# Choosing the tokens of eight experts: all at once before the expert stage, or one at a time, the next one's inside it

## The reference, cut to what matters

```python
logits = xf @ Wr + br                     # xf: 16384 x 512, 8 experts
Sm = softmax(logits, axis=-1)
G_t, idx_t = top_k(Sm.T, k)               # each expert takes its k = 16384/8 = 2048 best tokens
tokens = xf[idx]
mid = silu(einsum('keh,ehf->kef', tokens, W_up[group]) + b_up[group])   # F = 1365, a W_up for each pair of experts
out = einsum('kef,efh->keh', mid, W_down) + b_down
y = zeros_like(xf).at[idx].add(G[..., None] * out)
```

## Time and profile before

| | |
|---|---|
| time, median of 3 runs | 3380.66 us (3379.59 to 3381.59) |
| the profiled execution | 3389.43 us, of which 3387.7 us lie between its first and last instruction (the span) |
| PE busy | 3026.1 us, 89% of the span |
| DVE busy | 1734.5 us, 51% |
| ACT busy | 1279.6 us, 38% |
| POOL busy | 1204.9 us, 36% |
| mean granted TensorE clock | 0.953 |

### The profile page before, as it was taken

One profiled execution on the slowest core, in us unless ns is written; L12 is line 12 of the kernel. 1 busy time (PEld: TensorE's weight loads), 2 busy tenths in 40 slices (PEclk: granted clock), 3 DMA queues, 4 the chain that ended last, 5 costly groups with the idle time before them and its releaser, 6 DMA issues.

```text
span 3387.7 us, 58238 instructions
## 1 busy us (share of the span) xinstructions
PE 3026.1 (89%) x23738; PEld 2422.8 (72%) x23738; DVE 1734.5 (51%) x3966; ACT 1279.6 (38%) x2861; POOL 1204.9 (36%) x1100
## 2 busy tenths in 40 slices
PE   4898989989898710699999999999999999999998
PEld 3677777767677510588888888888888788788886
DVE  4788887888887759233333433333332333433432
ACT  4678787887878620111111211111211211211210
POOL 3556565565656433222222221222222222312221
PEclk8899999999999855799999999999999999999999
DMA  3233334333333230222322421322322313312311
GB/s 105 75 115 120 133 114 135 115 131 113 126 127 114 89 96 0 53 38 41 78 37 48 98 45 31 80 43 48 91 41 34 81 39 64 88 31 36 72 31 24
DMA packets 145476, 252.19 MB, mean 74 GB/s; under 512 B 35600, under 2 KB 36624, under 8 KB 145208
## 3 DMA queue, kind: packets, MB, share of 16 engines
q1 hardware_dynamic: 107432, 172.37, 15.2%
q0 software_dynamic: 32768, 67.72, 11.6%
q10 hardware_dynamic: 5008, 8.36, 0.9%
HBM read 137.82 MB, written 102.24 MB: 71 GB/s over the span
## 4 chain that ended last, share of the span: by engine, by line
PE 58%; DMA 1%; issue 0%; POOL 0%; DVE 0%; ACT 0%; POOLq 0%; ACTq 0%
PE UP L1446 28%; PE DN L1472 28%; PE TT L1429 2%; DMA w_raw<-in_L_ffn_W_down 0%; DMA idx<-list_scratch,slots 0%; DMA xg<-rows_scratch,idx 0%; POOL idx L1353 0%; POOL out_x L1378 0%; POOL xg L1362 0%; DVE down_lo L1070 0%; ACT z L1402 0%; ACT down_hi L1064 0%; DVE y L1517 0%; DVE xT_lo L1481 0%; DVE mid_lo L1499 0%
## 5 line engine op out<-in xcount | busy, mean ns | idle before, releaser
L1378 POOL DMA_INDIRECT out_x<-y,idx x128 | 202.0, 1578 | 1282.7 <-DVE y L1519 1282.7
L1402 ACT ACTIVATE z<-UP,bup 128x512 f32<-128x512 f32 (+1 forms) x352 | 240.9, 686 | 867.7 <-PE UP L1446 826.7
L1472 PE MATMUL DN<-down_hi,mid_hi 128*128 128x512 f32 x1408 | 566.7, 402 | 0.0
L1446 PE MATMUL UP<-xT_hi,up_lo 128*128 128x512 f32 (+1 forms) x1408 | 556.1, 395 | 0.0
L1446 PE MATMUL UP<-xT_hi,up_hi 128*128 128x512 f32 (+1 forms) x1408 | 553.6, 393 | 1.6 <-DVE xT_lo L1481 1.5
L1446 PE MATMUL UP<-xT_lo,up_hi 128*128 128x512 f32 (+1 forms) x1408 | 552.4, 392 | 0.0
L1472 PE MATMUL DN<-down_hi,mid_lo 128*128 128x512 f32 x1280 | 505.7, 395 | 0.0
L1472 PE MATMUL DN<-down_lo,mid_hi 128*128 128x512 f32 x1280 | 505.5, 395 | 0.0
L1517 DVE TENSOR_TENSOR y<-DN,bdn 128x512 f32<-128x512 f32 x128 | 88.5, 692 | 732.4 <-PE DN L1472 732.4
L1497 DVE CAST mid_hi<-z 128x512 fp32r<-128x512 f32 (+1 forms) x352 | 149.8, 426 | 504.8 <-ACT z L1402 504.8
L1389 ACT ACTIVATE xT_hi<-TT 128x512 fp32r<-128x512 f32 x128 | 76.4, 597 | 793.9 <-PE TT L1429 793.9
(11 more groups left out here) (244 smaller groups left out, 4974.8 us busy)
## 6 DMA issues: line engine op xcount, KB each, us to landing
xs<-in_x SPq DMA_DIRECT2D x32, 1024.0 KB, 8.2
kraw<-in_ctx SPq DMA_DIRECT2D x32, 1024.0 KB, 6.8
out_x<-xs SPq DMA_DIRECT2D x32, 1024.0 KB, 5.6
rows_scratch<-xfb SPq DMA_DIRECT2D x32, 1024.0 KB, 4.3
w_raw<-in_L_ffn_W_down SPq DMA_DIRECT2D x40, 512.0 KB
w_raw<-in_L_ffn_W_up SPq DMA_DIRECT2D x16, 682.5 KB
mid_hi<-mid_hi ACTq DMA_DIRECT2D x32, 86.0 KB
mid_lo<-mid_hi ACTq DMA_DIRECT2D x32, 84.0 KB
```

What stands on the lines that cost most here:

```text
L1378: pool.indirect_dma_start(out_rows, bass.IndirectOffsetOnAxis(ap=idx[:, n % 2, t:t + 1].bitcast(U32), axis=0), y[:, t, :], None, compute_o ...
L1402: act.activation(z[0:r, k % 2, :], UP[k % 3][0:r, :], ACT.Silu, bias=bup[0:r, e // 2, f:f + 1]).then_inc(s["z"], 1)
L1446: mm = pe.matmul(UP[k % 3][0:r, :], weights.up[wa][:, c, f * P:f * P + r], xT[xa][:, c, :], start=first, stop=(c == CH - 1 and wa == 1))
L1472: mm = pe.matmul(DN[m % 2][:, :], lhs, rhs, start=first, stop=(f == FCH - 1 and lhs is parts[-1][0]))
```

## The change

`choose` is gone, with its block, the two DRAM tensors and the lists of token numbers. A class `Select` inside `experts` chooses the tokens of one expert in 39 steps; a step is one PE part (`product`) and one DVE part (`decide`), which hand over to each other by the semaphores `asked` and `answered`. The gate values of one expert are 128x128, straight from a PE transpose of `sm_all`. The steps are: `turn`; 14 `upper` and 16 `lower` rounds; `ties`; `base` (how many were chosen in earlier partitions); and six `rows` steps, for three tiles of 128 slots each (the last for one). In a round PE multiplies the counts by a matrix of 2^40, so that the sum is far below or above, and DVE clamps it between the two possible next candidates (`ends`). In a `rows` step PE multiplies a 0/1 matrix (`within`: the partition in which a slot lies) by the places in order, and DVE counts how many places lie before the slot; that count is the token number, written to `slots` in SBUF.

The 39 steps of expert 0 stand at the start of the stage on PE and DVE. Those of expert e + 1 stand inside expert e's DN parts: at the chunks f = 2, 4, 6 and 8 of each `t`, so 16 in a block, in the expert's first three blocks. POOL now makes the constants, takes the `lo` of the first ten weight pieces, and only then gathers for block 0; its gathers and its adds to `out_x` take the token numbers from `slots`. SP's eight loads of biases now stand between the first two weight pieces and the other eight. ACT takes the ten `hi`, loads its table, turns the first rows, and then issues the three small moves of `lay`.

```diff
--- before
+++ after
+class Select:
...
+        self.steps = [("turn", 0)] + [("upper", k) for k in range(self.TOP_BIT - self.LOWER, -1, -1)] \
+            + [("lower", k) for k in range(self.LOWER - 1, -1, -1)] + [("ties", 0), ("base", 0)] \
+            + [("rows", g) for g in range(len(self.groups))]
...
+    def constants(self, pool):
+        step = Chain(pool, self.made)
+        step(pool.memset(self.huge[:, :], self.HUGE))
+        step(pool.memset(self.less[:, :], -float(self.K) / P))
+        step(pool.memset(self.less[0:1, :], 0.5 - float(self.K) / P))
+        step(pool.memset(self.ahead32[:, :], 1.0))
+        step(pool.tensor_copy(self.onesb[:, :], self.ahead32[:, :]))
+        step(pool.affine_select(out=self.ahead32[:, :], in_=self.ahead32[:, :], compare_op=ALU.is_gt, fill=0.0, base=0,
+                                pattern=[[1, P]], channel_multiplier=-1))
+        pool.tensor_copy(self.ahead[:, :], self.ahead32[:, :]).then_inc(self.made, 1)
+        pool.iota(self.places[:, P:P + 1], pattern=[[0, 1]], base=0, channel_multiplier=P, allow_small_or_imprecise_dtypes=True)
+        pool.iota(self.slot_end[:, :], pattern=[[P, self.KC]], base=1, channel_multiplier=1, allow_small_or_imprecise_dtypes=True)\
+            .then_inc(self.made, 1)
+        pool.iota(self.slot_row[:, :], pattern=[[1, self.K]], base=0, channel_multiplier=0, allow_small_or_imprecise_dtypes=True)\
+            .then_inc(self.made, 1)
+    def product(self, pe, e, i):
+        kind, g = self.steps[i]
+        bank, pc = self.bank, self.bank[:, 511:512]
+        if e or i:
+            pe.wait_ge(self.asked, len(self.steps) * e + i)
+        if kind == "turn":
+            mm = pe.transpose(bank[:, 0:P], self.sm_all[:, :, e], self.ident[:, :])
+        elif kind in ("upper", "lower"):
+            mm = pe.matmul(pc, self.huge[:, :], self.count[:, :], start=True, stop=True)
+        elif kind == "ties":
+            pe.matmul(pc, self.onesb[:, :], self.tot[:, :], start=True, stop=False)
+            mm = pe.matmul(pc, self.ahead[:, :], self.ties[:, :], start=False, stop=True)
+        elif kind == "base":
+            mm = pe.matmul(pc, self.ahead[:, :], self.taken[:, :], start=True, stop=True)
+        else:
+            for j in range(len(self.groups[g])):
+                mm = pe.matmul(bank[:, j * (P + 1):(j + 1) * (P + 1)], self.within[g % 2][:, j * P:(j + 1) * P], self.places[:, :],
+                               start=True, stop=True)
+        mm.then_inc(self.answered, 1)
+    def reach(self, dve, values, cand, bit):
+        dve.tensor_scalar(self.hit[:, :], values, cand[:, :], self.less[:, :], ALU.is_ge, ALU.add, accum_out=self.count[:, :])\
+            .then_inc(self.asked, 1)
+        half = float(1 << (bit - 1)) if bit else 0.0
+        dve.tensor_scalar(self.ends[:, 0:1], cand[:, :], -half if bit else -1.0, None, ALU.add)
+        self.step(dve.tensor_scalar(self.ends[:, 1:2], cand[:, :], half, None, ALU.add))
+    def lie_within(self, dve, g):
+        first, n = self.groups[g][0] * P, len(self.groups[g]) * P
+        row = self.slot_row[:, first:first + n]
+        self.step(dve.tensor_scalar(self.begun[:, 0:n], row, self.base[:, :], None, ALU.is_ge))
+        return dve.scalar_tensor_tensor(out=self.within[g % 2][:, 0:n], in0=row, scalar=self.past[:, :], in1=self.begun[:, 0:n],
+                                        op0=ALU.is_lt, op1=ALU.mult)
+    def decide(self, dve, e, i):
+        kind, g = self.steps[i]
+        bank, pc = self.bank, self.bank[:, 511:512]
+        if self.step is None:
+            self.step = Chain(dve, self.own)
+        step = self.step
+        halves = self.V[:, :].bitcast(U16)
+        upper, lower = halves[:, 1:2 * P:2], halves[:, 0:2 * P:2]
+        dve.wait_ge(self.answered, len(self.steps) * e + i + 1)
+        if kind == "turn":
+            step(dve.memset(self.cand[0][:, :], float(1 << (self.TOP_BIT - self.LOWER))))
+            step(dve.tensor_copy(self.V[:, :], bank[:, 0:P]))
+            if e == 0:
+                dve.wait_ge(self.made, 3)
+            self.reach(dve, upper, self.cand[0], self.TOP_BIT - self.LOWER)
+        elif kind in ("upper", "lower"):
+            old, new = self.cand[(i - 1) % 2], self.cand[i % 2]
+            step(dve.tensor_scalar(new[:, :], pc, self.ends[:, 0:1], self.ends[:, 1:2], ALU.max, ALU.min))
+            if g:
+                self.reach(dve, upper if kind == "upper" else self.key[:, :], new, g - 1)
+            elif kind == "upper":
+                dve.tensor_copy(self.low[:, :], new[:, :])
+                step(dve.scalar_tensor_tensor(out=self.key[:, :], in0=upper, scalar=new[:, :], in1=lower, op0=ALU.is_equal, op1=ALU.mult))
+                step(dve.tensor_scalar(self.beyond[:, :], upper, new[:, :], float((1 << self.LOWER) - 1), ALU.is_gt, ALU.mult))
+                step(dve.memset(new[:, :], float(1 << (self.LOWER - 1))))
+                step(dve.tensor_tensor(self.key[:, :], self.key[:, :], self.beyond[:, :], ALU.add))
+                self.reach(dve, self.key[:, :], new, self.LOWER - 1)
+            else:
+                step(dve.tensor_scalar(self.low32[:, 0:1], self.low[:, :], float(1 << self.LOWER), None, ALU.mult))
+                step(dve.tensor_copy(self.low32[:, 1:2], new[:, :]))
+                step(dve.tensor_tensor(self.low32[:, 0:1], self.low32[:, 0:1], self.low32[:, 1:2], ALU.bitwise_or))
+                least = self.low32[:, 0:1].bitcast(FP32)
+                step(dve.tensor_scalar(self.over[:, :], self.V[:, :], least, 0.0, ALU.is_gt, ALU.add, accum_out=self.tot[:, :]))
+                dve.tensor_scalar(self.same[:, :], self.V[:, :], least, 0.0, ALU.is_equal, ALU.add, accum_out=self.ties[:, :])\
+                    .then_inc(self.asked, 1)
+                dve.wait_ge(self.asked, len(self.steps) * e + i + 1)
+                step(dve.tensor_tensor_scan(self.rank[:, :], self.same[:, :], self.same[:, :], 0.0, ALU.add, ALU.bypass))
+        elif kind == "ties":
+            step(dve.tensor_scalar(self.need[:, :], pc, -1.0, float(self.K), ALU.mult, ALU.add))
+            step(dve.scalar_tensor_tensor(out=self.same[:, :], in0=self.rank[:, :], scalar=self.need[:, :], in1=self.same[:, :], op0=ALU.is_le, op1=ALU.mult))
+            step(dve.tensor_tensor(self.over[:, :], self.over[:, :], self.same[:, :], ALU.add))
+            step(dve.tensor_tensor_scan(self.rank[:, :], self.over[:, :], self.over[:, :], 0.0, ALU.add, ALU.bypass))
+            dve.tensor_copy(self.taken[:, :], self.rank[:, P - 1:P]).then_inc(self.asked, 1)
+        elif kind == "base":
+            step(dve.tensor_copy(self.base[:, :], pc))
+            if e == 0:
+                dve.wait_ge(self.made, self.MADE)
+            step(dve.tensor_tensor(self.past[:, :], self.base[:, :], self.rank[:, P - 1:P], ALU.add))
+            step(dve.tensor_scalar(self.places[:, 0:P], self.rank[:, :], self.base[:, :], None, ALU.add))
+            self.lie_within(dve, 0).then_inc(self.asked, 1)
+            dve.wait_ge(self.asked, len(self.steps) * e + i + 1)
+            step(self.lie_within(dve, 1))
+        else:
+            for j, b in enumerate(self.groups[g]):
+                at = j * (P + 1)
+                ins = dve.tensor_scalar(self.early[:, j, :], bank[:, at:at + P], self.slot_end[:, b:b + 1], bank[:, at + P:at + P + 1],
+                                        ALU.is_lt, ALU.add, accum_out=self.token[:, b:b + 1])
+            ins.then_inc(self.asked, 1)
+            dve.wait_ge(self.asked, len(self.steps) * e + i + 1)
+            a, b = self.groups[g][0], self.groups[g][-1] + 1
+            dve.tensor_copy(self.slots[:, e * self.KC + a:e * self.KC + b], self.token[:, a:b]).then_inc(self.ids, 1)
+            if g + 2 < len(self.groups):
+                step(self.lie_within(dve, g + 2))
+    def listed(self, n):
+        e, last = n * TILES // self.KC, (n * TILES + TILES - 1) % self.KC
+        return len(self.groups) * e + last // 3 + 1
...
+        SELECT_AT = (2, 4, 6, 8)
+        def next_steps(n, t):
+            e, first = n // BPE + 1, ((n % BPE) * 4 + t) * len(SELECT_AT)
+            return {f: first + j for j, f in enumerate(SELECT_AT) if e < NEXP and first + j < len(select.steps)}
...
             def _(sp):
                 full = (FCH - 1) * P
+                for m in range(2):
+                    weights.load(sp, m)
                 with nc.allow_non_contiguous_dma(reason="biases by partition, once"):
                     for g in range(NEXP // 2):
                         sp.dma_start(bup[:, g, 0:FCH - 1], io["bup"][g, 0:full].rearrange("(c p) -> p c", p=P)).then_inc(s["bup"], 16)
                         sp.dma_start(bup[0:FLAST, g, FCH - 1:FCH], io["bup"][g, full:FDIM].unsqueeze(1)).then_inc(s["bup"], 16)
+                for m in range(2, first_down):
+                    weights.load(sp, m)
                 m = first_down
...
-                def list_rows(n):
-                    if n >= 2:
-                        for t in range(4):
```

(54 more changed lines are left out.)

206 lines of the change are left out of this document (30 added, 176 removed).

## The result

The changed kernel takes 3335.66 us, median of four runs (3332.43 to 3337.72), against 3380.68 (3379.59 to 3381.59) beside it: ratio 0.9866, interval 0.9849 to 0.9883, so 1.3% less, clear of the noise. The forecast was 3334.6, in 3300 to 3378. Its profiled execution took 3335.54 us.

A forecast was written before the change was run, and what follows sets the result against it. PE's stream was taken to bound the expert stage, and the choice the time ahead of it. -120.4 + 48.7 + 25.6 = -46.1 us gave 3343 profiled, median 3334.6, range 3300 to 3378.

The forecast's parts named there:

- What bounds the kernel: Expert stage: PE's stream and its waits are paid in full, DVE and POOL work is free; ahead, only the choice counts.
- Part 1: Choice before the first block: first UP at 1266.7 instead of 1387.09, gain 120.4 us, bounds 102 to 124.
- The round: Each of expert 0's 30 search rounds: 0.28 + 0.14 + 0.22 + 0.19 = 0.83 us, 24.9 in all.
- Stalls behind POOL: Front choice: `key`, tie steps and `lie_within`, with two SBUF inputs, wait for POOL operations; 5 us taken, tokens at 1252.
- A: Front choice: `ends` stall behind POOL, tokens at 1266, first UP 1280.7, gain 106.4, median 3348.6; chance 0.18.
- The `bup` loads: SP's queue ahead of the first gather: they delay POOL's ten `lo` by 3 us (0 to 5), POOL free at 1253.
- Part 2: 7 x 39 steps inside PE's expert-stage stream: 48.7 us own cost plus 25.6 us waits.
- A product: Among DN matmuls: 0.15 us each (0.07 to 0.42); with 1.1 for wider ones, 6.95 an expert, 48.7 in all.
- C: DN parts: each product empties PE's pipe and leaves the load open, 0.42 us; +28, 3408.9; chance 0.12.
- B: DN parts: products cost 0.07 us and DVE answers faster, waits 17 us; -79, 3301; chance 0.20.
- Waits: PE waits on DVE at `key`, last round, base, rows 0, 1, 3, 4: 3.65 us an expert, 25.6 (10 to 45).
- D: Expert stage: DVE work isn't hidden, waits at every product, some 0.3 us; +56 on the forecast, about 3391; chance 0.08.

## Why the prediction was right, step by step

**What bounds the kernel** held: everything put into PE's stream was paid, and DVE's and POOL's own work beside it cost nothing (first UP to end without steps 2000.5 against 2000.6; PE busy 499.96 of 500 with 254 us of DVE beside it).

**Part 1, the choice: predicted -120.4, measured -116.2.**
- The round was to take 0.83 and took 1.09, 7.8 us in thirty. This is the term that was mis-sized most. Its parts were 0.28, 0.14, 0.22, 0.19 and came out 0.33, 0.15, 0.29, 0.32. I took `hit` and the clamp at the price of the same shapes in the earlier trace rows, which have one scalar or constants. `hit` now reads two scalars for each partition from SBUF, and the clamp two as well: 0.28 us against 0.16 for L1237 of the earlier trace rows, same size, from PSUM too. For `hit` an edit shows it (346 ns with one scalar, 405 with two); for the clamp it is a comparison with another operation. PE's answer, 0.29 for 0.22, stays open: the runs show only that it goes with the operation that reads it, since `base`'s copy, which reads no scalar, starts 0.22 after its product. (The prediction's 0.28 for `hit` also rests on 896 columns at 1.06 ns being 0.93 us; they are 0.95.)
- Stalls behind POOL: 5 us assumed, about 2.7 measured (L1213 2.26, L1218 0.42).
- With these, tokens come 43.4 + 7.8 - 2.3 = 48.9 after the start; measured 48.2.
- `ends` never stalled, so A is out, and its price was nearly right: two elements wide they cost 12.8 us where A had 14.0. The prediction's rule from the Trainium skill ("Advanced Engine Details and Errata", VectorE Performance Modes) wants an outer dimension that is even, or odd and above 1. The traces agree: one element (240 of 240 pass) and two elements (held up to 2805 ns) fall on its two sides.
- The `bup` loads in SP's queue: 3 us taken, nothing found. POOL had its ten `lo` at 1245.08, 39.8 after the start, and I had 44.4. So not POOL but DVE set the first gather, by 8.7 us; that turn was not foreseen, since the two errors had opposite signs.
- Gather to rows 7.7 (7.35), landing to UP 6.1 (6.1).

**Part 2, the steps inside: predicted +74.3, measured +65.6.**
- A product 0.125 instead of 0.15, and all products 38.2 instead of 48.7, by the kernel that has them alone. C (0.42) and B (0.07 each) are out: without a wait the pipe doesn't empty. DN starts lie 0.27 apart across a product and then 0.31, where the pace is 0.233; 0.38 at once was forecast. The 0.125 splits into 0.027 for the product and 0.10 around it. By the Trainium skill ("TensorE: Matmul & The Clock Gate", LDWEIGHTS (loading the stationary operand)) a load of 128 columns comes to about 107 ns (an estimate, 128 / 1.2), and by the section "Wait — 56ns, not 53.3ns?" matmuls, however narrow, start no less than about 25 ns apart. The traces agree on the second with 0.027, and on the first with 0.10 us for the load of `huge` (at 1306.05 in the changed kernel); the DN weights' load behind it takes 0.20, so the page's figure doesn't hold for that one. Which load stands open no run shows.
- Waits 27.5 instead of 25.6, at the seven steps named. From DN start to DN start, less what the kernel with the products alone has there (0.28 for one product, 0.30 at the ties, 0.40 for three products of 129 columns), expert 2's waits are 0.78 for `key` (0.55 predicted), 0.46 at the ties' product, behind the last round (0.25), and 0.43 behind base (0.45); behind the rows steps 0, 1, 3 and 4 they are 0.50, 0.58, 0.56 and 0.25 (0.5, 0.7, 1.0 and 0.2). That makes 3.56, where the prediction had 3.65; the same steps' listed idle times are only 2.4, which fits a last matmul recorded at 0.39 or 0.40 us where the pace is 0.233: some 0.16 of each wait is counted as busy. So this part was right step by step, but `key` and the last round were put too short and rows 3 too long, which nearly cancels. Of the 27.5, 3.9 for each expert, the rest is not traced to a step. Spacing them took the waits away.
- D is out: DVE rose to 251 of 500 us, and yet the products of the rounds have no wait on it but at `key` and at the last round.

**The sum.** By stages the changed kernel gained 50.6 us, and 46.1 was forecast: an error of +4.2 and one of -8.7, which partly cancel. That the median came within 1.1 us of the forecast is luck. The profiled execution was forecast at 3343 and took 3335.5, 7.8 less: 4.5 by the stages and 3.3 by the attention stage, whose end varies by more than that from execution to execution. The 8.8 us that were then taken off, because the profiled execution before lay that far above its median, had no counterpart after, where it lay within 0.2 us of its median.

## What to carry to other kernels

A serial choice or search can be hidden in a stream of wide matmuls for some 0.125 us a step, if between asking and using an answer lies more matmul time than the slowest answer takes: give the few long answers wider places rather than all steps the same. Price a small step by the nearest row with the same number of per-partition scalars, not by shape alone. And where a gain lies in a stretch that stalls behind another engine's long operations, shifting it may only move the stall: 0.06 us taken from each of 30 rounds, 1.8 in all, brought the first UP less than 0.1 us forward.

## What the runs showed that I had not expected

- A scalar that a DVE operation reads per partition from SBUF costs about 0.06 us: `hit` 346 ns with one and 405 with two. Two 128x1 operations that read PSUM fit this, 158 ns with constants (L1237 of the earlier trace rows) and 278 with two scalars, though they aren't the same operation.
- A DVE operation that POOL holds up waits to the end of POOL's operation, whatever its own size: 2.32 us for two elements with one input, 2.55 for 128 with two. One element, or 128 with an accumulated count (`hit`), are not held up.
- A wait of PE inside a stream of wide matmuls costs more than the idle time listed for it: 0.78 us for 0.62.
- The end of an attention stage that is the same in all kernels lay between 1195.2 and 1209.95 us, more than most differences looked at here. Lengths within a trace tell edits apart that whole times can't.
